# A graph layer on one core: who makes the bf16 parts of three pieces of x, and fewer constant matmuls in the loop

## The reference

```python
x: (3125, 128) f32; 53125 edges sorted by dst; edge_attr: (53125, 128); W1: (128, 256); W2: (256, 128)
msg   = x[src] + edge_attr
neigh = segment_sum(msg, dst, num_segments=3125)
rst   = (1 + eps) * x + neigh
h     = rst @ W1 + b1
h     = relu((h - mean(h)) * rsqrt(var(h) + 1e-5) * gamma + beta)     # statistics over the nodes
out   = layernorm(x + h @ W2 + b2)                                    # over the 128 features
```

## Time and profile before

| | |
|---|---|
| median of the runs | 260.47 us |
| the profiled execution, its own time | 260.06 us |
| its span, first to last instruction | 258.2 us |
| busy PE, DVE, ACT, POOL | 242.8, 186.1, 128.4, 175.9 us |
| PE matmul share of the span | 94% |
| constant matmuls (line 674) | 75 |

### The profile page before, as it was taken

One profiled execution on the slowest core, in us unless ns is written; L12 is line 12 of the kernel. 1 busy time (PEld: TensorE's weight loads), 2 busy tenths in 40 slices (PEclk: granted clock), 3 DMA queues, 4 the chain that ended last, 5 costly groups with the idle time before them and its releaser, 6 DMA issues.

```text
span 258.2 us, 6778 instructions
## 1 busy us (share of the span) xinstructions
PE 242.8 (94%) x2171; PEld 201.1 (78%) x2171; DVE 186.1 (72%) x686; ACT 128.4 (50%) x228; POOL 175.9 (68%) x116
## 2 busy tenths in 40 slices
PE   7959879999999999999999999999999999999970
PEld 3747768889989987888888888878878889745970
DVE  4988868798888887878878777777658311288872
ACT  2333543454556564555554554544444330376793
POOL 4298888888888888888888888888888810450000
PEclk9986999999999999999999999999999999999995
DMA  2997657788788888888887778877767410000044
GB/s 66 276 321 132 147 101 161 172 201 178 174 200 207 189 204 178 184 196 209 183 188 169 180 173 187 182 180 163 155 129 166 74 20 3 0 0 3 3 124 129
DMA packets 51342, 38.13 MB, mean 148 GB/s; under 512 B 5099, under 2 KB 51099, under 8 KB 51305
## 3 DMA queue, kind: packets, MB, share of 16 engines
q1 hardware_dynamic: 36445, 30.89, 41.2%
q0 software_dynamic: 14400, 6.56, 21.2%
q10 hardware_dynamic: 460, 0.21, 0.3%
HBM read 36.05 MB, written 1.60 MB: 146 GB/s over the span
## 4 chain that ended last, share of the span: by engine, by line
PE 85%; DVE 6%; ACT 3%; issue 2%; DMA 1%; DVEq 1%; ACTq 1%
PE ps L757 29%; PE ps L765 21%; PE ps L796 11%; PE ps L790 7%; PE ps L737 4%; PE ps L870 4%; PE ps L674 3%; PE ps L856 2%; PE ps L787 2%; DMA big<-in_dst_dram 1%; PE ps L726 1%; ACT big L658 1%; DVE hit_k L1049 1%; DVE hit_l L1042 1%; ACT big L616 1%
## 5 line engine op out<-in xcount | busy, mean ns | idle before, releaser
L523 POOL DMA_INDIRECT egat<-in_x_dram,srci x100 | 166.1, 1661 | 38.1 <-issue 28.6
L616 ACT ACTIVATE big<-ps 128x500 f32 x158 | 96.4, 610 | 103.8 <-PE ps L796 73.6
L765 PEld LDWEIGHTS ps<-hit_c,ebuf 128*128 128x128 f32 x632 | 101.2, 191 | 10.9 <-DVE aggT L1134 3.6
L765 PE MATMUL ps<-hit_c,ebuf 128*128 128x20 f32 x632 | 94.9, 228 | 2.9 <-DVE aggT L1134 2.7
L1134 DVE TENSOR_TENSOR aggT<-aggT,ps 128x20 f32 x208 | 36.0, 173 | 49.7 <-PE ps L765 33.9
L757 PE MATMUL ps<-big,xN 128*128 128x120 f16 (+7 forms) x200 | 58.0, 292 | 1.5 <-ACT aggT L591 1.5
L757 PE MATMUL ps<-big,xr 128*128 128x120 f16 (+7 forms) x200 | 58.1, 292 | 0.0
L757 PE MATMUL ps<-big,x_room 128*128 128x120 f16 (+7 forms) x200 | 58.1, 292 | 0.0
L796 PE MATMUL ps<-hit_k,hit_l 128*128 128x375 f16 x158 | 54.0, 342 | 0.0
L790 PE MATMUL ps<-hit_k,hit_l 128*128 128x300 f16 x158 | 45.7, 290 | 0.0
L1049 DVE TENSOR_TENSOR hit_k<-iota_b,key 128x752 f16<-128x752 f16 x79 | 43.0, 544 | 0.0
(11 more groups left out here) (109 smaller groups left out, 212.7 us busy)
## 6 DMA issues: line engine op xcount, KB each, us to landing
ebuf<-in_edge_attr_dram SPq DMA_DIRECT2D x79, 256.0 KB
egat<-in_edge_attr_dram SPq DMA_DIRECT2D x49, 128.0 KB
egat<-in_x_dram,srci POOLq DMA_INDIRECT x100
xN<-in_x_dram SPq DMA_DIRECT2D x6, 256.0 KB, 4.1
out_dram<-big SPq DMA_DIRECT2D x5, 256.0 KB
w_sb<-in_L_gnn_W_dram SPq DMA_DIRECT2D x2, 128.0 KB
out_dram<-big SPq DMA_DIRECT2D x2, 128.0 KB
big<-in_src_dram ACTq DMA_DIRECT2D x1, 192.0 KB
```

Source lines behind the costliest of these rows:

```text
L523: return nc.gpsimd.indirect_dma_start(to, None, x[:, :], bass.IndirectOffsetOnAxis(ap=ix, axis=0), compute_op=op)
L616: nc.scalar.activation(cnt[:, :, bass.ds(lows[m % LOADS], WIN)], ps[:, m % BANKS_C, 0:KEYS].rearrange("p (t n) -> p t n", n=WIN), ACT.Copy ...
L765: last = nc.tensor.matmul(ps[:, SUMS + w % BANKS_S, 0:WIN], rows_v[:, j * D:(j + 1) * D], hits_v, start=(j == 0), stop=(j == ROWS - 1))
```

## The change

- The x pieces 4, 5 and 3 get their parts from TensorE and ScalarE. `sum_rest` sums ident @ x (f32, 512 columns) and minus @ upper(x) (bf16, 512 columns) in PSUM, and ScalarE stores that as `xr`; `sum_last` adds minus @ upper(xr), and ScalarE stores that as `x3`. They stand in windows 3, 8, 15 and 5, 10, 17. `minus` is the identity times -1 in bf16.
- VectorE makes the parts of pieces 0, 1, 2 and 6 alone, `rest` in windows 3, 6, 10, 14 and `part_3` a window later.
- The transposes of a piece stand in one window, 2i for the i-th (two in either half), all in one PSUM bank (`ACC`), so each piece waits for the scaling of the one ahead of it. The other bank takes the sums.
- `fill` in the loop: 1 in each of the counted groups 0 and 1, none after. Ahead of the loop 15, 2, 1 and 4 in place of 14, 3, 2 and 6; the first 15 read a tile that VectorE sets.
- Loads: only the first three x pieces, two chunks and one slot are issued ahead of the loop; the others, slots 1 to 6 and chunk 2 on, wait for windows. The weights are issued in window 40.
- Start: `dst` is complete after 4 transfers in place of 5 (the `nexts` load has its own semaphore); `firsts` is loaded by SP and clamped in three parts; the src turn comes ahead of the key turn; b2 is copied by ScalarE; key and lo are copied by one instruction each; `hit_k` comes ahead of `hit_l`; the first register load takes 4 groups.
- The tests of the index lists move: their result is shared in window 60 in place of 46; a memset of part of `cnt` moves from the start to window 45.
- Worked out from `arrange()` with the new `HITS`: windows 6, 9 and 12 are gathered among the first 13, then 15, 19, 24, 29. The last seven places are the same but for one window.

```diff
-SPREAD = 3
-X_RATE = 2
+X_LEAD = 2
+SLOTS_W = (0, 2, 5, 7, 10, 13)
+SPLITS_W = (3, 6, 10, 14)
+RESTS_W = (3, 8, 15)
-HITS = 3000
+HITS = 3200
-FILL_HEAD = 14
-FILL_KEY = 3
-FILL_LO = 2
-FILL_CARRY = 6
-FILLS = ((10, 3), (20, 2))
+FILL_HEAD = 15
+FILL_KEY = 2
+FILL_LO = 1
+FILL_CARRY = 4
+FILLS = ((2, 1),)
+LOAD_0 = 4
...
+        X_AT = [2 + X_LEAD * i for i in range(NB - 3)]
+        SLOT_AT = list(SLOTS_W)
+        CHUNK_AT = [max(CHUNK * (c - CHUNKS) + CHUNK - 1, min(CHUNK * (c - 2), c + 1)) for c in range(2, GC // CHUNK)]
+        SUM_B = [early_g, early_g + 1, early_g - 1]
+        SPLIT_B = [b for b in range(NB) if b not in SUM_B]
+        LAST_AT = [w + 2 for w in REST_AT]
+        TURN_AT = [2 * i for i in range(NB)]
...
@@ SyncE
-            sp.wait_ge(dst_loaded, 80)
+            sp.wait_ge(dst_loaded, 64)
             sp.wait_ge(src_loaded, 64)
             chunk(0)
+            slot(0)
             x_piece(X_ORDER[0])
-            slot(0)
...
             for w in range(G):
+                if w in X_AT:
+                    sp.wait_ge(window_summed, w + 1)
+                    x_piece(X_ORDER[3 + X_AT.index(w)])
+                if w in SLOT_AT:
+                    sp.wait_ge(window_summed, w + 1)
+                    slot(1 + SLOT_AT.index(w))
...
@@ ScalarE
+                    if store_of(REST_AT[i]) == m:
+                        act.wait_ge(x_rest_summed, i + 1)
+                        nc.scalar.activation(xr[:, t0:t1, :], ps[:, ACC + 1, :].rearrange("p (t d) -> p t d", d=D),
+                                             ACT.Copy).then_inc(x_rest_stored, 1)
+                    if store_of(LAST_AT[i]) == m:
+                        act.wait_ge(x_last_summed, i + 1)
+                        nc.scalar.activation(x3[:, t0:t1, :], ps[:, ACC + 1, :].rearrange("p (t d) -> p t d", d=D),
+                                             ACT.Copy).then_inc(x_last_stored, 1)
...
@@ TensorE
+            def sum_rest(i):
...
+                if i > 0:
+                    pe.wait_ge(x_last_stored, i)
+                nc.tensor.matmul(ps[:, ACC + 1, :], ident[:, :], xN[:, t0:t1, :].rearrange("p t d -> p (t d)"),
+                                 start=True, stop=False, skip_group_check=True)
+                nc.tensor.matmul(ps[:, ACC + 1, :].rearrange("p (t d) -> p t d", d=D), minus, upper(xN[:, t0:t1, :]),
+                                 start=False, stop=False, skip_group_check=True).then_inc(x_rest_summed, 1)
+            def sum_last(i):
...
+                pe.wait_ge(x_rest_stored, i + 1)
+                nc.tensor.matmul(ps[:, ACC + 1, :].rearrange("p (t d) -> p t d", d=D), minus, upper(xr[:, t0:t1, :]),
+                                 start=False, stop=True, skip_group_check=True).then_inc(x_last_summed, 1)
...
-                turn_x(X_RATE * w, X_RATE * w + 1)
+                if w in TURN_AT:
+                    turn_x(TURN_AT.index(w), 0)
+                if w in REST_AT:
+                    sum_rest(REST_AT.index(w))
+                if w in LAST_AT:
+                    sum_last(LAST_AT.index(w))
...
@@ VectorE
-                if w % SPREAD == 1 and w // SPREAD < NB:
-                    rest(w // SPREAD)
-                    part_3(w // SPREAD)
+                if w in SPLIT_AT:
+                    rest(SPLIT_B[SPLIT_AT.index(w)])
+                if w - 1 in SPLIT_AT:
+                    part_3(SPLIT_B[SPLIT_AT.index(w - 1)])
```

More of the change, by code:

```diff
@@ L459, in _ @@
                         slot(G_OF[w] + SLOTS)
[L460 removed]
+                elif C_OF[w] in CHUNK_AT:
                     sp.wait_ge(window_summed, w + 1)
[L462 removed]
+                    chunk(2 + CHUNK_AT.index(C_OF[w]))
+                if w == W_WEIGHTS:
+                    sp.dma_start(w1_sb[:, :], w1).then_inc(weights_loaded, 16)
+                    sp.dma_start(w2_sb[:, :, :], w2.rearrange("(h p) d -> p h d", p=P)).then_inc(weights_loaded, 16)
+                    for k, v in enumerate((b1, gamma, beta)):
+                        sp.dma_start(col[:, k, :], v.rearrange("(h p) -> p h", p=P),
+                                     allow_slow_non_contiguous=True).then_inc(weights_loaded, 16)
             sp.wait_ge(path_known, 1)
@@ L609, in _ @@
                     lows = [nc.snap(r, donate=True, min_val=0, max_val=CNT - WIN) for r in regs]
+                for i in range(len(SUM_B)):
+                    t0, t1 = pieces(SUM_B[i])
+                    if store_of(REST_AT[i]) == m:
[6 more added lines that the diff above has]
+                                             ACT.Copy).then_inc(x_last_stored, 1)
+                for i in range(NB):
+                    if store_of(TURN_AT[i]) == m and C_AT[m] > TURN_AT[i]:
+                        scale_x(i, x_turned, x_scaled, ps[:, ACC, :])
                 act.wait_ge(counts_made, m + 1)
@@ L669, in _, with fill @@
         def _(pe):
-            def fill(bank, n):
+            def fill(bank, n, v=iota_b[:, :]):
                 for _ in range(n):
-                    nc.tensor.matmul(ps[:, bank, 0:KEYS_B], iota_b[:, 0:P], iota_b[:, 0:KEYS_B], start=True, stop=True,
+                    nc.tensor.matmul(ps[:, bank, 0:KEYS_B], v[:, 0:P], v[:, 0:KEYS_B], start=True, stop=True,
                                      skip_group_check=True)
+            pe.wait_ge(head_filler_made, 1)
+            fill(0, FILL_HEAD, hit_k[:, RING_K - 1, :])
+            pe.wait_ge(ident_made, 1)
             pe.wait_ge(filler_made, 1)
-            fill(0, FILL_HEAD)
-            pe.wait_ge(ident_made, 1)
             def turn(bank, v, n):
@@ L693, in _ @@
             turn(2, lambda k: rel_v[:, k // ROWS, k % ROWS, :], HJ).then_inc(rel_turned, 1)
-            pe.wait_ge(row_loaded, 32)
-            pe.wait_ge(constants_made, 2)
-            nc.tensor.matmul(ps[:, 6, 0:D + 1], ones[0:1, :], row[0:1, :], start=True, stop=True).then_inc(b2_shared, 1)
+            pe.wait_ge(src_rows_made, 1)
+            turn(7, lambda k: src_v[:, k // ROWS, k % ROWS, :], HJ).then_inc(src_turned, 1)
             fill(0, FILL_KEY)
@@ L702, in _ @@
             turn(4, lambda k: lo_v[:, k, :], HJ).then_inc(lo_turned, 1)
-            pe.wait_ge(src_rows_made, 1)
-            turn(7, lambda k: src_v[:, k // ROWS, k % ROWS, :], HJ).then_inc(src_turned, 1)
+            pe.wait_ge(row_loaded, 32)
+            pe.wait_ge(constants_made, 2)
+            nc.tensor.matmul(ps[:, 6, 0:D + 1], ones[0:1, :], row[0:1, :], start=True, stop=True).then_inc(b2_shared, 1)
             fill(0, FILL_CARRY)
@@ L709, in _, with turn_x @@
             last.then_inc(carry_turned, 1)
-            def turn_x(n0, n1):
-                for n in range(n0, min(n1, NT)):
-                    i, t = X_TILES[n]
-                    t0, t1 = pieces(X_ORDER[i])
+            def turn_x(i, half):
+                b = X_ORDER[i]
+                t0, t1 = pieces(b)
+                if half == 0:
+                    pe.wait_ge(x_loaded[b], 16)
+                    pe.wait_ge(key_made, 1)
+                    if i > 0:
+                        pe.wait_ge(x_scaled, i)
+                for t in range(t0 + 2 * half, min(t0 + 2 * half + 2, t1)):
@@ L925, in _ @@
         def _(dve):
+            nc.vector.memset(hit_k[:, RING_K - 1, :], 1.0).then_inc(head_filler_made, 1)
             nc.vector.memset(top[:, :], float(WIN - 1)).then_inc(bounds_made, 1)
```

191 lines of the change are left out of this document (106 added, 85 removed).

## The result

The changed kernel takes 262.37 us (median of 6 runs, 261.89 to 263.71) against 260.35 for the kernel before on the same chip: a ratio of 1.0103 with the interval 1.0073 to 1.0134. It is slower by 1%, where 254.5 was forecast. The profiled execution took 262.25, its span is 260.5. In all that follows a median is over every execution of a kernel, while a ratio leaves out executions more than 1.5% above the kernel's fastest, so the two need not match (least of all in `e_mild`, where that takes out six of ten).

The account below looks back on a forecast made before the run. TensorE was taken to bound the kernel from 36 us, with a race against VectorE before. From 260.06, 6.9 gained up to the first multiply less 1.1 lost behind it gave 254.3, or 254.5 adjusted towards the median; range 251.2 to 260.2.

Parts of the forecast that it names:

- Ahead of the loop: Start of the kernel: the new order gains 0.6 us, so the first hits end at 11.2 in place of 11.83.
- VectorE's work, windows 0 to 12, and the stall at window 3: Early loop: VectorE sets the pace, the stall shrinks, and the first multiply moves from 35.76 to 28.9, 6.9 us gained.
- TensorE's waits for ScalarE behind turned pieces: Windows 0 to 12: 0.4 us of waiting per pair of windows, hidden by VectorE's 1.35 a window; 2.5 if VectorE were fast.
- Behind window 13: After the first multiply: fewer fills gain 2.9 us, the third piece costs 1.3, VectorE's lateness 2.4; net 1.1 lost.
- Transfers and gathers: From 11 to 20 us: spread loads shorten two gathers towards 1.54 us, and the third gather starts near 14, not 18.01.
- Rival 5: VectorE is relieved but the SP queue or gathers bind; ends within 2 us of the forecast, counted in its chance.
- the slack: At the last gather: 4.9 us of slack and 4 gained by an earlier third gather cover the 5.8 that TensorE gains.
- The clock: First 13 windows: with no pause expected above 1.2 us, the clock stays up, at 1.00 over 11 to 60 us.
- the prediction's own sign of being wrong: Clock row at 0.50 behind 18 us, or TensorE waiting for adds beyond window 35, would show the forecast wrong.
- 18 fills go, 2.9 us: Behind window 13: removing 18 fills of counted groups 11 to 19, at 0.16 us each, gains 2.9 us.
- rivals 3 and 4: Clock at 1.2 GHz from about 17 until window 13, 259.6, chance 0.15; from 11 to about 40, 264.7, chance 0.11.
- The rule on transposes: Early windows: transposes don't engage the full clock, so thinned windows with 25 of them would run at 1.2 GHz.

Follow-up runs that it names:

- e_mild: The kernel after with 24 constant matmuls (fills) in the loop in place of 2, nothing else changed: 259.90 us, ratio 0.9914.
- e_pause: The kernel after with VectorE waiting for the first scaled piece of x ahead of its third set of hits: 257.69 us, ratio 0.9909.
- p_mild: The kernel after with VectorE's pause ahead of its third set of hits and 24 fills in place of 2: 255.60 us, ratio 0.9845.
- p_fills: The kernel after with VectorE's pause ahead of its third set of hits and the 50 old fills in place of 2: 258.16 us, ratio 0.9946.
- b_fills: The kernel before with only the loop fills of the kernel after, one in each of counted groups 0 and 1: 272.06 us, ratio 1.0460.
- p_again: p_mild repeated unchanged beside the kernel before: 255.98 us, ratio 0.9840.
- g_late: The kernel after with the first two gathered windows moved from 6 and 9 to 8 and 10: 258.61 us, ratio 0.9936.
- v_gap: The kernel after with VectorE's wait for the carries moved ahead of the first key hits, so it pauses near 10 us: 258.32 us, ratio 0.9907.
- v_mild: The kernel after with VectorE's wait for the carries ahead of the first key hits and 24 fills in place of 2: 257.67 us, ratio 0.9903.
- e_wait: The kernel after with GpSimd's first gather waiting for the sum of window 1: 262.64 us, ratio 1.017.
- v_issue: The kernel after with VectorE waiting, ahead of the scalar_tensor_tensor of the carries, until GpSimd reaches its first gather: 262.80 us, ratio 1.0091.

## Why the prediction was wrong

**Ahead of the loop**: right. First hits end at 10.43 + 0.41 = 10.84, forecast 11.2; in `e_pause`, which has the same code up to there, at 11.41.

**VectorE's work, windows 0 to 12, and the stall at window 3**: right as a mechanism. VectorE runs from 8.56 to 18.78 without a break, and the gap of 2.75 is gone. In `p_mild`, where the two failures below are mended, the first multiply stands at 30.36, with a pause of 1.0 and 16 more fills in its early windows, against a forecast of 28.9: 5.4 gained in place of 6.9. (`e_pause`, with a pause of 0.7 and no more fills, has 30.16.) TensorE's waits for ScalarE behind turned pieces, which were put in VectorE's shade, are bare there, 1.4; the 0.8 ahead of the multiply was right, 0.87.

**Behind window 13**: in `p_mild` the last block's multiply is 180.72 behind the first, before 179.65: 1.07 lost, forecast 1.1. That agreement is luck, two misses that cancel. `p_fills`, with 14 more fills behind window 13, has 213.18 - 31.06 = 182.12, so these 14 cost 1.40, 0.10 each, where the prediction took 0.16; and with all 18 fills of before the third piece, the one window more counted and VectorE's lateness together cost 182.12 - 179.65 = 2.5, where it added 1.3, 0.3 and 2.4 to 4.0. With all 18 gone the kernel after lost 3.5, the second cold stretch in it.

**Transfers and gathers**: this step failed first. "The two gathers of 2.00 and 4.01 us there fall towards 1.54" became 9.65 and 1.85, and the "third gather near 14" was issued at 21.53. I had put the 4.01 of the earlier trace rows down to the loads, with the DMA share above 1. It has 0.53 and 0.75 there now, and the gather is longer. The better reading was in the same rows: 13.70 + 4.01 - 1.55 = 16.16, just before the first of VectorE's two operations on piece 0 ends and the second, which waits for it, starts. (`b_fills` repeats it: 13.44 + 4.00 - 1.55 = 15.89, and its second operation starts at 16.05.) What the change did was to make VectorE's run unbroken, which was its merit in my sum, and to issue the gather 0.18 behind the start of L1178, the last instruction for 8 us that had to wait for another. Rival 5 had named the gathers, but within 2 us of the forecast.

The Trainium skill, "SBUF — State Buffer", "Who interferes with whom", says that a VectorE instruction with two SBUF inputs contends with a GpSimd instruction that reads SBUF. The rows of the held gathers agree with that (hits have two SBUF inputs, the gather reads its list there, and it is let go where the run breaks), but the hold of 8 us in the kernel after goes over 24 instructions, and the gathers that got in within a run are not explained by it. Where the page infers that such operations leave descriptor making alone, the held gathers don't bear it out. That VectorE's pause sets the end of a held gather is shown by six profiles that agree to 0.12 us, two places of the pause among them; that the order at 9.4 decides rests on profiles that differ by chance, not on an edit.

The forecast also had the slack wrong. It looked at the last gather, where nothing was lost (it is issued at 209.13 and TensorE doesn't wait). The first was the one that mattered: before, window 7 was the first gathered one; now it is window 6, and TensorE reaches it at 18.1, where it read its first gathered rows at 26.6 before.

**The clock**: "the longest pause that I expect is 1.2. So by the rows it stays up" failed in both halves, and the prediction's own sign of being wrong, 0.50 behind 18 us, came true. The 4.89 took it down once. The second fall, 35 to 42, and the one that `e_pause` keeps, come behind pauses none of which is over 0.9: the earlier trace rows, with 1.00 over a pause of 1.49, was no proof, since before had its fills around that pause. Removing the first cause gave 4.7 (262.37 to 257.69; 5.0 by the ratios), 24 fills in place of 2 gave 2.1 on top (to 255.60; 1.7 by the ratios), and together they end 1.1 from the forecast. "18 fills go, 2.9 us" is the mis-sized term that goes with it: 14 of them were worth 1.40, and with 22 fewer than `p_mild` has, the last 4 of these 18 among them, the way from the first multiply to the last block's grew from 180.72 in `p_mild` to 183.33 in `e_pause`, 2.6 lost to the clock. The time lies between rivals 3 and 4 (259.6 and 264.7), and neither is what happened: the clock was low for 7 us from within the stall on, high again, and low for 7 more. The rule on transposes, weighed in the prediction, isn't what happened: the loop from 11 to 18.1, with transposes and hardly a fill among its matmuls, has 1.00.

## What to carry to other kernels

Before you make an engine's run gapless, ask who lived in its gaps. Here an indirect gather of GpSimd that was issued just behind the last gap of VectorE's run had to wait for the next one, and one deliberate pause of 0.7 to 1.0 us ahead of the first reader's deadline was worth 4.7 us. Constant matmuls should be cut only after the pauses that they bridge are gone, and to the number that keeps the clock (24 here; with 2 `e_pause` lost it in nine of ten executions, and 50 cost 2.6 us of their own). The version with both, `p_again`, beats both kernels: 255.98, ratio 0.984.

## What the runs showed of the hardware

- A gather of 1.55 us took up to 9.74 (`g_late`) beside VectorE's run of f16 comparisons; others issued within such a run took 1.67 (`v_gap`), 1.79 (`v_mild`) and 1.97 (`e_wait`). The difference is not explained.
- The clock stayed at 1.2 GHz through stretches with TensorE busy all the time: 15.00 of 15.00 from 45 to 60 in `b_fills`.
- The clock fell in `e_pause` behind a stretch with 7.62 busy of 10.00 and no wait over 0.9, and held in `p_mild` with 9.03 of 10.00.
- An engine that waits for what another has just passed isn't behind that other's instruction: GpSimd's gather was recorded 0.22 behind the VectorE instruction that waited for GpSimd to reach it (`v_issue`).
